# Layer 0's message sum: the one-hots of every fourth group made by ScalarE in place of VectorE

## Chip, core and metric

One core of a Trainium2 chip runs the whole program. The metric is the device time of one execution in microseconds (us); lower is better.

## What is computed

The program is two graph layers over N = 6250 nodes (256 features) and E = 100000 edges. Layer 0 is an attention with six kinds of edges, layer 1 an attention over all edges and self loops. The change lies in one step of layer 0, the sum of weighted messages into their target nodes. In the reference it is this (`w` is the softmax weight, one per edge and head, and the sum over relations follows):

```python
hsum = jax.ops.segment_sum(w[:, :, None] * val_e, seg, num_segments=S)
...
t = (t_rel * present[..., None].astype(x.dtype)).sum(1) / nrel[:, None]
```

`w * val_e` has 256 numbers per edge (4 heads of 64), and the weights themselves are summed as 4 more columns.

## The kernel before, in words

Edges are sorted by target node and cut into visits. A visit is 256 edges (two tiles of 128) that all add into one block of 128 nodes; there are 440 visits. `sum_messages` works on turns of 16 tiles, so 8 visits (t = 0 to 7) in 4 groups (g = 0 to 3) of four tiles, and there are 55 turns. The first turn is written out, the other 54 are a hardware loop. In each turn:

- **SP** loads the value rows of each group, 128x1024 numbers, into `vrows` (line 1174). A group's buffer is loaded again as soon as its values have been weighed, and the four groups are loaded in order, so the load of g = 1 stands behind that of g = 0, and g = 3 behind g = 2.
- **Weigh** (line 1157) multiplies the rows by the weights into `wv`. VectorE weighs groups 0 and 2, GpSimd groups 1 and 3. It waits for the load and for TensorE to be done with the same group of the turn before, since `wv` has one buffer per group.
- **Hot** (line 1263) makes the one-hots of the group's four tiles on VectorE: a 128x512 comparison of a ramp (`iota`) with each edge's place in its block (`dr`). It goes to `vhot`.
- **Beside** (line 1184) copies the weights into the last columns of `wv` on ScalarE.
- **Visit** (line 1237) is two accumulating matmuls of a one-hot (128x128) with weighed rows (128x260, fp32) into one of four PSUM banks. Visit t waits for hot, weigh and beside of its group, in this order, and then for the add of visit t-4, which frees its bank.
- **Add** (line 1256) puts a visit's bank onto the running sum, on VectorE: `run = run * same + psM`. It waits for the visit and for the add before it.
- **Keep** (line 1196) copies each running sum into the accumulator of its node block, on ScalarE.

The order is written out by hand in each engine's program. On VectorE a turn is: weigh 0, hot 0, adds 4 and 5 of the turn before, hot 1, adds 6 and 7 of the turn before, weigh 2, hot 2, adds 0 and 1, hot 3, adds 2 and 3. On ScalarE: beside 0, keeps 4 and 5 (turn before), beside 1, keeps 6 and 7 (turn before), beside 2, keeps 0 and 1, beside 3, keeps 2 and 3. GpSimd does weigh 1 and weigh 3 alone. A hot of one turn may be overwritten once the visits of its group in the turn before are done (`m_done`).

Layer 1 already makes its one-hots on ScalarE in two steps, |dr - ramp| (line 1780) and relu(1 - that) (line 1788). The edge scores of layer 0 do likewise (lines 886 and 889).

Of the kernel before, what the change touches and what calls it, by code (L numbers as in the profile page):

```python
# [6 lines left out]
P = 128  # L7
# [26 lines left out]
ACT = mybir.ActivationFunctionType  # L34
AX = mybir.AxisListType
ds, ts = bass.ds, bass.ts
# [740 lines left out]
GS = 4  # L777
SLOTS = 4 * GS
# [346 lines left out]
def sum_messages(nc, c, dr, v, layer, weights, nh, acc):  # L1125
# [5 lines left out]
    V8 = SLOTS // 2  # L1131
    with Stage(nc) as tmp:
        def sb(name, shape, dt=F32):
            return tmp.enter_context(nc.sbuf_tensor(f"{name}{L}", shape, dt))

        def sem(name):
            return tmp.sem(f"{name}{L}")
# [2 lines left out]
        rows = sb("vrows", [P, SLOTS, D])  # L1140
        wv = sb("wv", [P, SLOTS, width])
        hot = sb("vhot", [P, SLOTS, P])
        run = sb("run", [P, V8, MSG])
        psW = tmp.enter_context(nc.psum_tensor(f"psW{L}", [P, 2, 1024], F32))
        psM = tmp.enter_context(nc.psum_tensor(f"psM{L}", [P, 4, 512], F32))
        w_in = [sem("w_in0_"), sem("w_in1_")]
        loaded = [sem(f"loaded{g}_") for g in range(4)]
        wv_done = [sem("wv_even_"), sem("wv_odd_")]
        w_tr, w_out, ww_done, hot_done, m_done, run_done, kept = map(sem, (
            "w_tr", "w_out", "ww_done", "vhot_done", "m_done", "run_done", "sum_kept"))  # L1150
        NG = SLOTS // GS

        def weigh(engine, ops, i, g):

            engine.wait_ge(loaded[g], 16 * (i + 1))
            engine.wait_ge(m_done, i * V8 + 2 * g + 2)
            ops.tensor_tensor(  # L1157
                wv[:, g * GS:(g + 1) * GS, 0:D].rearrange("p k (h d) -> p k h d", h=H),
                rows[:, g * GS:(g + 1) * GS].rearrange("p k (h d) -> p k h d", h=H),
                w[:, ts(i * NG + g, GS), 0:H].unsqueeze(3).to_broadcast([P, GS, H, DK]), ALU.mult).then_inc(wv_done[g % 2], 1)  # L1160

        with nc.Block() as block:
            @block.sync
            def _(sp):
                for t in range(CT):
                    if t >= 2:
                        sp.wait_ge(w_tr, t - 1)
                    sp.dma_start(win[:, t % 2], weights.rearrange("h (t c p) -> t c h p", t=CT, p=P)[t]).then_inc(w_in[t % 2], 16)
                with sp.Fori(0, NI) as i:
                    for g in range(NG):  # L1170

                        sp.wait_ge(wv_done[g % 2], i * (NG // 2) + g // 2 + 1)
                        o = dr["val"].rearrange("(i k p) d -> i p k d", k=GS, p=P)[ds(i * NG + g, 1)]
                        sp.dma_start(rows[:, g * GS:(g + 1) * GS], o.rearrange("o p k d -> (o p) k d")).then_inc(loaded[g], 16)

            @block.scalar
            def _(act):
                act.sem_inc(kept, V8)
                act.wait_ge(w_out, CT)

                def beside(i, g):

                    act.wait_ge(m_done, i * V8 + 2 * g + 2)
                    nc.scalar.copy(wv[:, g * GS:(g + 1) * GS, D:width], w[:, ts(i * NG + g, GS)]).then_inc(ww_done, 1)

                regs = [act.alloc_register(f"sblk{t}") for t in range(4)]

                def keep(i, visits):
                    if visits[0] % 4 == 0:
                        act.load(regs, v["blk"][0:1, ds(i * V8 + visits[0], 4)])  # L1190
                    for t in visits:
                        V = i * V8 + t
                        blk = act.snap(regs[t % 4], min_val=0, max_val=NB - 1)
                        act.wait_ge(run_done, V + 5)
                        act.wait_ge(kept, V + V8)
                        nc.scalar.copy(acc[:, ds(blk, 1)].rearrange("p o d -> p (o d)"), run[:, t]).then_inc(kept, 1)  # L1196

                def turn(i, first=False):

                    for g in range(NG):  # L1200
                        beside(i, g)
                        if g >= 2:
                            keep(i, (2 * g - 4, 2 * g - 3))
                        elif not first:
                            keep(i - 1, (2 * g + 4, 2 * g + 5))
                turn(0, True)
                with act.Fori(1, NI) as i:
                    turn(i)
                keep(NI - 1, range(4, V8))

            @block.gpsimd
            def _(pool):
                pool.sem_inc(wv_done[1], NG // 2)
                pool.wait_ge(w_out, CT)
                with pool.Fori(0, NI) as i:
                    for g in range(1, NG, 2):
                        weigh(pool, nc.gpsimd, i, g)

            @block.tensor
            def _(pe):  # L1220
                pe.sem_inc(m_done, V8)
                for t in range(CT):
                    pe.wait_ge(w_in[t % 2], 16 * (t // 2 + 1))
                    if t >= 2:
                        pe.wait_ge(w_out, t - 1)
                    for h in range(nh):
                        ins = nc.tensor.transpose(psW[:, t % 2, h * P:h * P + CW], win[:, t % 2, h], c["ident"][0:CW, 0:CW])
                    ins.then_inc(w_tr, 1)
                with pe.Fori(0, NI) as i:
                    for t in range(V8):  # L1230
                        if t % 2 == 0:
                            pe.wait_ge(hot_done, i * NG + t // 2 + 1)
                            pe.wait_ge(wv_done[t // 2 % 2], (i + 1) * (NG // 2) + t // 4 + 1)
                            pe.wait_ge(ww_done, i * NG + t // 2 + 1)
                        pe.wait_ge(run_done, i * V8 + t + 1)
                        for j in range(2):
                            ins = nc.tensor.matmul(psM[:, t % 4, 0:width], hot[:, 2 * t + j], wv[:, 2 * t + j], start=(j == 0), stop=(j == 1))  # L1237
                        ins.then_inc(m_done, 1)

            @block.vector  # L1240
            def _(dve):
                dve.sem_inc(wv_done[0], NG // 2)
                for t in range(CT):
                    dve.wait_ge(w_tr, t + 1)
                    nc.vector.tensor_copy(w[:, t * CW:(t + 1) * CW].rearrange("p c h -> p h c"),
                                          psW[:, t % 2].rearrange("p (h c) -> p h c", c=P)[:, 0:nh, 0:CW]).then_inc(w_out, 1)
                dve.sem_inc(run_done, 3)
                nc.vector.memset(run[:], 0.0).then_inc(run_done, 1)
                dve.wait_ge(w_out, CT)

                def add(i, t):
                    V = i * V8 + t
                    dve.wait_ge(m_done, V + 1 + V8)
                    dve.wait_ge(run_done, V + 4)
                    dve.wait_ge(kept, V + 1)
                    nc.vector.scalar_tensor_tensor(out=run[:, t, 0:width], in0=run[:, (t - 1) % V8, 0:width], scalar=v["same"][:, ds(V, 1)],  # L1256
                                                   in1=psM[:, t % 4, 0:width], op0=ALU.mult, op1=ALU.add).then_inc(run_done, 1)
                def turn(i, first=False):
                    for g in range(NG):
                        if g % 2 == 0:  # L1260
                            weigh(dve, nc.vector, i, g)
                        dve.wait_ge(m_done, i * V8 + 2 * g + 2)
                        nc.vector.tensor_tensor(hot[:, g * GS:(g + 1) * GS], c["iota"][:].unsqueeze(1).to_broadcast([P, GS, P]),  # L1263
                                                v["dr"][:, ts(i * NG + g, GS)].unsqueeze(2).to_broadcast([P, GS, P]),
                                                ALU.is_equal).then_inc(hot_done, 1)

                        if g >= 2:
                            add(i, 2 * g - 4)
                            add(i, 2 * g - 3)
                        elif not first:  # L1270
                            add(i - 1, 2 * g + 4)
                            add(i - 1, 2 * g + 5)
                turn(0, True)
                with dve.Fori(1, NI) as i:
                    turn(i)
                for t in range(V8 - 4, V8):
                    add(NI - 1, t)
# [973 lines left out]
```

## Time and profile before

| | us |
|---|---|
| median of 3 runs | 4758.05 |
| lowest and highest run | 4743.52, 4765.12 |
| profiled execution, its own time | 4761.29 |
| its span in the trace | 4758.8 |
| the sum of layer 0 in it, first weigh to last add | 2365.8 to 2948.4 |

The span is the time from the first to the last instruction. PE is TensorE (PEld its weight loads), DVE is VectorE, ACT is ScalarE, POOL is GpSimd, SP issues the loads. Busy time is counted per instruction, and a name like L1263 is a line of the kernel before. In the timeline a row is one instruction or a run of equal ones (x2, x8); a visit shows as 4 matmul rows, so x8 is two visits.

### The profile page before, as it was taken

The page shows a single profiled execution, that of the slowest core. Times are in us where ns is not written, and L with a number is a line of the kernel's source. Part 1 is how long each engine was busy: PE and PEld are TensorE (multiplying, and loading weights), DVE is VectorE, ACT ScalarE, POOL GpSimd, SP SyncE. Part 2 cuts the span into 40 slices and gives each one's busy share as a digit, 9 for nine tenths or more (in the row PEclk, how much of TensorE's full clock was granted, in tenths as well). Part 3 has the DMA queues.
Part 4 walks back from the last instruction along what each step waited for, and adds up shares of the span by engine and source line. Part 5 has one row for each costly group of instructions (what it writes and reads, how often), then busy time and mean ns, then how long its engine had stood idle before and what let it go on. Part 6 is the DMA issues. An engine that isn't in the chain of part 4 may idle for free. (4 is left out here: it accounts for less than half of the span.)

```text
span 4758.8 us, 56459 instructions
## 1 busy us (share of the span) xinstructions
PE 2853.5 (60%) x10779; PEld 1822.5 (38%) x10780; DVE 3061.9 (64%) x6090; ACT 1481.4 (31%) x3656; POOL 2084.0 (44%) x2102
## 2 busy tenths in 40 slices
PE   0799997666666674000177776766355666556632
PEld 0455554433334342000155554434244444445421
DVE  5333334555555554999899998676366666666665
ACT  0122223333333332231033333434234433434302
POOL 1000005777777774000033333222577777777550
PEclk9999998777877777555599999899677777777765
DMA  4344447999999997000155554000466666666531
GB/s 154 111 137 137 140 140 253 315 312 316 315 314 315 314 315 247 0 0 0 66 197 200 201 196 151 15 18 17 108 188 193 191 185 191 192 189 193 158 122 54
DMA packets 648045, 815.90 MB, mean 171 GB/s; under 512 B 155094, under 2 KB 552310, under 8 KB 647602
## 3 DMA queue, kind: packets, MB, share of 16 engines
q1 hardware_dynamic: 532228, 457.32, 30.0%
q0 software_dynamic: 115696, 357.28, 24.7%
q8 instruction: 38, 0.62, 0.1%
q14 instruction: 83, 0.68, 0.0%
HBM read 541.33 MB, written 274.25 MB: 171 GB/s over the span
## 5 line engine op out<-in xcount | busy, mean ns | idle before, releaser
L821 POOL DMA_INDIRECT rows<-kv,kvi x880 | 832.7, 946 | 890.9 <-DVEq L893 623.0
L1721 POOL DMA_INDIRECT g_rows<-x1t,srci x880 | 848.8, 965 | 286.3 <-issue 259.4
L866 PE MATMUL psD<-qs,hot 128*128 x1760 | 702.9, 525 | 247.7 <-DVE prod L907 193.3
L907 DVE TENSOR_TENSOR prod<-rows,psD 128x256 f32<-128x256 f32 x880 | 363.6, 417 | 465.4 <-DMA rows<-kv,kvi 353.9
L1875 PE MATMUL g_psM<-g_rows,g_hot 128*128 128x264 f32 x1760 | 570.8, 479 | 77.5 <-DVE g_rows L1993 71.0
L1157 POOL TENSOR_TENSOR wv<-vrows,wgt 128x1024 f32<-128x1024 f32 x110 | 219.5, 1996 | 840.0 <-DMA vrows<-val_v 622.3
L866 PEld LDWEIGHTS psD<-qs,hot 128*128 128x128 f32 x1760 | 381.6, 252 | 521.0 <-issue 309.6
L1237 PE MATMUL psM<-wv,vhot 128*128 128x260 f32 x1760 | 445.7, 397 | 138.4 <-DVE run L1256 131.5
L1875 PEld LDWEIGHTS g_psM<-g_rows,g_hot 128*128 128x128 f32 x1760 | 390.0, 233 | 171.9 <-issue 94.2
L1237 PEld LDWEIGHTS psM<-wv,vhot 128*128 128x128 f32 x1760 | 318.1, 190 | 265.9 <-DVE run L1256 219.3
L886 ACT ACTIVATE off<-psB,npiota 128x256 f32<-128x256 f32 x440 | 207.7, 472 | 669.8 <-PE psB L857 667.8
L901 DVE TENSOR_REDUCE sc<-prod 128x4 f32<-128x256 f32 x880 | 357.3, 411 | 0.0
L733 PE MATMUL psKV<-wkv,hT 128*128 128x512 f32 x588 | 302.3, 596 | 0.0
L1788 ACT ACTIVATE g_hot<-g_far 128x512 f32<-128x512 f32 x220 | 138.5, 630 | 520.1 <-PE g_psZ L1864 474.3
L1196 ACT COPY acc<-run 128x264 f32 x440 | 181.3, 412 | 367.7 <-DVE run L1256 366.9
L1780 ACT ACTIVATE g_far<-iota,dr 128x128 f32<-128x128 f32 x880 | 278.0, 386 | 14.8 <-PEq L69 14.8
L1993 DVE TENSOR_TENSOR g_rows<-g_rows,g_psW 128x1024 f32<-128x1024 f32 x220 | 265.6, 1207 | 0.0
L1929 DVE TENSOR_REDUCE g_e<-g_psD 128x128 f32<-128x384 f32 x55 | 30.6, 557 | 361.9 <-DMA g_rows<-x1t,srci 361.9
L1885 PE MATMUL g_psZ<-ident,g_z 128*64 128x128 f32 x55 | 23.0, 418 | 381.7 <-DVE g_z L1935 359.2
L1256 DVE SCALAR_TENSOR_TENSOR run<-run,same,psM 128x260 f32<-128x260 f32 x440 | 211.0, 480 | 35.2 <-DVE run L1256 12.3
L685 DVE COPY qs<-psQ 128x256 f32 (+1 forms) x49 | 20.8, 425 | 329.8 <-PE psQ L737 329.8
L1263 DVE TENSOR_TENSOR vhot<-iota,dr 128x512 f32<-128x512 f32 x220 | 232.0, 1055 | 0.0
(359 smaller groups left out, 4634.8 us busy)
## 6 DMA issues: line engine op xcount, KB each, us to landing
val_v<-rows SPq DMA_DIRECT2D x220, 512.0 KB, 5.0
vrows<-val_v SPq DMA_DIRECT2D x220, 512.0 KB
kv<-stage SPq DMA_DIRECT2D x98, 768.0 KB, 4.7
sums_v<-g_run SPq DMA_DIRECT2D x110, 528.0 KB, 3.6
g_drow<-drow_v SPq DMA_DIRECT2D x55, 512.0 KB
rows<-kv,kvi POOLq DMA_INDIRECT x880, 5.0
g_rows<-x1t,srci POOLq DMA_INDIRECT x880
g_ndt<-nodeb SPq DMA_DIRECT2D x440, 6.0 KB
```

The costliest lines, as they stand in the source:

```text
L733: mm(psKV[:], hT[:, m % 2, t, g], wkv[:, g, t], start=(t == 0 and g == 0), stop=False)
L821: nc.gpsimd.indirect_dma_start(out=rows[:, k], out_offset=None, in_=table, in_offset=bass.IndirectOffsetOnAxis(ap=index[:, i * SLOTS + k:i ...
L866: nc.tensor.matmul(psD[:, k % 4, 0:cols], hot[:, t % 2, j * P:(j + 1) * P], node[:, ds(blk[t], 1)].rearrange("p o d -> p (o d)"), start=Tr ...
L901: nc.vector.tensor_reduce(sc[:, k], prod[:, k % 4].rearrange("p (h d) -> p h d", h=H), AX.X, ALU.add).then_inc(sc_done, 1)
L907: ins = nc.vector.tensor_tensor(prod[:, k % 4], rows[:, k, 0:D], psD[:, k % 4, 0:D], ALU.mult)
L1157: ops.tensor_tensor(wv[:, g * GS:(g + 1) * GS, 0:D].rearrange("p k (h d) -> p k h d", h=H), rows[:, g * GS:(g + 1) * GS].rearrange("p k (h ...
L1237: ins = nc.tensor.matmul(psM[:, t % 4, 0:width], hot[:, 2 * t + j], wv[:, 2 * t + j], start=(j == 0), stop=(j == 1))
L1263: nc.vector.tensor_tensor(hot[:, g * GS:(g + 1) * GS], c["iota"][:].unsqueeze(1).to_broadcast([P, GS, P]), v["dr"][:, ts(i * NG + g, GS)]. ...
L1721: nc.gpsimd.indirect_dma_start(out=rows[:, i % NBUF, k, 0:ROW1], out_offset=None, in_=dr["x1t"], in_offset=bass.IndirectOffsetOnAxis(ap=v[ ...
L1780: ins = nc.scalar.activation(far[:, n % 2, k], c["iota"][:], ACT.Abs, scale=-1.0, bias=v["dr"][:, K:K + 1])
L1875: ins = nc.tensor.matmul(psM[:, V % 4, 0:MSG], hot[:, 2 * t + j], rows[:, i % NBUF, 2 * t + j], start=(j == 0), stop=(j == 1))
L1993: tt(out, out, w.unsqueeze(3).to_broadcast([P, GRP, H, DK]), ALU.mult).then_inc(wv_done, 1)
```

## The change

ScalarE makes the one-hots of group 3 of each turn, by a new function `places`; VectorE no longer does hot 3. `places` writes |dr - ramp| of four tiles into a new buffer `vfar`, one tile at a time (128x128 each), waits for its own last write and for TensorE's visits of the turn before, and then writes relu(1 - vfar) for the group at once (128x512). It stands on ScalarE ahead of beside 2. TensorE waits for a semaphore of its own before visits 6 and 7.

```diff
+        far = sb("vfar", [P, GS, P])
...
+                def places(i):
+                    g = NG - 1
+                    for k in range(GS):
+                        ins = nc.scalar.activation(far[:, k], c["iota"][:], ACT.Abs, scale=-1.0, bias=v["dr"][:, ds(i * SLOTS + (g * GS + k), 1)])
+                    ins.then_inc(far_done, 1)
+                    act.wait_ge(far_done, i + 1)
+                    act.wait_ge(m_done, i * V8 + 2 * g + 2)
+                    nc.scalar.activation(hot[:, g * GS:(g + 1) * GS], far[:], ACT.Relu, bias=1.0, scale=-1.0).then_inc(last_hot, 1)
+
                 def turn(i, first=False):
 
                     for g in range(NG):
+                        if g == 2:
+                            places(i)
                         beside(i, g)
...
-                            pe.wait_ge(hot_done, i * NG + t // 2 + 1)
+                            if t // 2 < NG - 1:
+                                pe.wait_ge(hot_done, i * (NG - 1) + t // 2 + 1)
+                            else:
+                                pe.wait_ge(last_hot, i + 1)
...
-                        dve.wait_ge(m_done, i * V8 + 2 * g + 2)
-                        nc.vector.tensor_tensor(hot[:, g * GS:(g + 1) * GS], c["iota"][:].unsqueeze(1).to_broadcast([P, GS, P]),
+                        if g < NG - 1:
+                            dve.wait_ge(m_done, i * V8 + 2 * g + 2)
+                            nc.vector.tensor_tensor(hot[:, g * GS:(g + 1) * GS], c["iota"][:].unsqueeze(1).to_broadcast([P, GS, P]),
```

```order
L1195 REGISTER_ALU
L1196 ISA
L1196 COPY acc<-run 128x264
L1183 REGISTER_ALU
L1184 ISA
L1184 COPY wv<-wgt 128x4x4
```

The same place with the change, from the last of the four vfar steps to beside 2:

```order
L1202 ISA
L1202 ACTIVATE vfar<-iota,dr 128x128
L1204 REGISTER_ALU
L1205 REGISTER_ALU
L1206 ACTIVATE vhot<-vfar 128x512
L1184 REGISTER_ALU
L1185 ISA
L1185 COPY wv<-wgt 128x4x4
```

Five engine instructions now stand between keep 7 and beside 2: four vfar steps and one vhot step.

VectorE in the loop, before, from add 1 to add 2 (vhot is hot 3):

```order
L1256 SCALAR_TENSOR_TENSOR run<-run,same,psM 128x260
L1262 REGISTER_ALU
L1263 ISA
L1263 TENSOR_TENSOR vhot<-iota,dr 128x512
L1253 REGISTER_ALU
L1255 REGISTER_ALU
L1256 ISA
L1256 SCALAR_TENSOR_TENSOR run<-run,same,psM 128x260
```

The same place with the change:

```order
L1271 SCALAR_TENSOR_TENSOR run<-run,same,psM 128x260
L1268 REGISTER_ALU
L1270 REGISTER_ALU
L1271 ISA
L1271 SCALAR_TENSOR_TENSOR run<-run,same,psM 128x260
```

Add 2 follows add 1 directly; adds 0 to 3 are now four in a row.

## Rows read from the trace of the kernel before

**Rows 1.** Page of the kernel before: totals by engine; granted TensorE clock in 40 slices.
```profile
PE 2853.5 (60%) x10779; PEld 1822.5 (38%) x10780; DVE 3061.9 (64%) x6090; ACT 1481.4 (31%) x3656; POOL 2084.0 (44%) x2102
...
PEclk9999998777877777555599999899677777777765
```

**Rows 2.** Windows view, inside the sum: us, busy of PE, PEld, DVE, ACT, POOL; clock, DMA, GB/s.
```profile
2600.00:2650.00 50.00, 38.29 (x153) 27.20 (x153) 46.38 (x68) 18.05 (x57) 19.34 (x10) 1.00 0.57 192
```

**Rows 3.** Groups by line within the sum of layer 0: busy us, mean ns | idle before, releaser.
```profile
L1263 DVE TENSOR_TENSOR vhot<-iota,dr 128x512 f32<-128x512 f32 x220 | 232.0, 1055 | 0.0
```

**Rows 4.** Timeline of one turn of the sum: start us, us, instruction [idle before <-releaser].
```profile
2599.54 1.22 DVE L1157 TENSOR_TENSOR wv<-vrows,wgt 128x1024 f32<-128x1024 f32 x1
...
2600.68 0.68 DVE L1263 TENSOR_TENSOR vhot<-iota,dr 128x512 f32<-128x512 f32 x1
...
2601.06 2.07 POOL L1157 TENSOR_TENSOR wv<-vrows,wgt 128x1024 f32<-128x1024 f32 x1 [3.22 <-PE psM L1237]
...
2602.39 1.28 DVE L1263 TENSOR_TENSOR vhot<-iota,dr 128x512 f32<-128x512 f32 x1
...
2603.60 1.10 DVE L1256 SCALAR_TENSOR_TENSOR run<-run,same,psM 128x260 f32<-128x260 f32 x2
...
2604.12 2.02 PE L1237 MATMUL psM<-wv,vhot 128*128 128x260 f32 x8 [0.29 <-DVE run L1256]
...
2604.61 1.22 DVE L1157 TENSOR_TENSOR wv<-vrows,wgt 128x1024 f32<-128x1024 f32 x1
2604.89 0.41 ACT L1196 COPY acc<-run 128x264 f32 x1 [0.21 <-DVE run L1256]
2605.21 0.20 ACT L1184 COPY wv<-wgt 128x16 f32 x1
...
2606.35 1.10 DVE L1256 SCALAR_TENSOR_TENSOR run<-run,same,psM 128x260 f32<-128x260 f32 x2
2606.44 1.90 POOL L1157 TENSOR_TENSOR wv<-vrows,wgt 128x1024 f32<-128x1024 f32 x1 [3.31 <-PE psM L1237]
...
2606.88 2.02 PE L1237 MATMUL psM<-wv,vhot 128*128 128x260 f32 x8 [0.74 <-DVE run L1256]
...
2607.36 1.53 DVE L1263 TENSOR_TENSOR vhot<-iota,dr 128x512 f32<-128x512 f32 x1
...
2608.81 1.09 DVE L1256 SCALAR_TENSOR_TENSOR run<-run,same,psM 128x260 f32<-128x260 f32 x2
...
2609.34 2.02 PE L1237 MATMUL psM<-wv,vhot 128*128 128x260 f32 x8 [0.44 <-DVE run L1256]
...
2610.05 1.22 DVE L1157 TENSOR_TENSOR wv<-vrows,wgt 128x1024 f32<-128x1024 f32 x1
...
2611.61 2.03 POOL L1157 TENSOR_TENSOR wv<-vrows,wgt 128x1024 f32<-128x1024 f32 x1 [3.26 <-PE psM L1237]
...
2616.96 1.90 POOL L1157 TENSOR_TENSOR wv<-vrows,wgt 128x1024 f32<-128x1024 f32 x1 [3.33 <-DMA vrows<-val_v]
```

**Rows 5.** Timeline, start of the sum: a weigh of VectorE beside one of GpSimd.
```profile
2376.68 1.90 POOL L1157 TENSOR_TENSOR wv<-vrows,wgt 128x1024 f32<-128x1024 f32 x1 [4.82 <-PE psM L1237]
2376.94 2.72 DVE L1157 TENSOR_TENSOR wv<-vrows,wgt 128x1024 f32<-128x1024 f32 x1
```

**Rows 6.** Timeline, layer 1: the same two ScalarE steps.
```profile
3965.18 1.26 ACT L1780 ACTIVATE g_far<-iota,dr 128x128 f32<-128x128 f32 x4
...
3966.47 0.63 ACT L1788 ACTIVATE g_hot<-g_far 128x512 f32<-128x512 f32 x1
```

**Rows 7.** Timeline, layer 0's scores: ScalarE's Abs, Relu, and the matmul behind them.
```profile
1713.82 0.47 ACT L886 ACTIVATE off<-psB,npiota 128x256 f32<-128x256 f32 x1 [3.42 <-PE psB L857]
...
1714.41 0.42 ACT L889 ACTIVATE hot<-off 128x256 f32<-128x256 f32 x1
...
1715.06 1.13 PE L866 MATMUL psD<-qs,hot 128*128 x4 [1.11 <-ACT hot L889]
```

**Rows 8.** Timeline, last turn of the sum: four visits in one go.
```profile
2943.90 3.77 PE L1237 MATMUL psM<-wv,vhot 128*128 128x260 f32 x16 [0.74 <-DVE run L1256]
```

More of the change, by code:

```diff
@@ L1148, in sum_messages @@
         wv_done = [sem("wv_even_"), sem("wv_odd_")]
-        w_tr, w_out, ww_done, hot_done, m_done, run_done, kept = map(sem, (
-            "w_tr", "w_out", "ww_done", "vhot_done", "m_done", "run_done", "sum_kept"))
+        w_tr, w_out, ww_done, hot_done, far_done, last_hot, m_done, run_done, kept = map(sem, (
+            "w_tr", "w_out", "ww_done", "vhot_done", "vfar_done", "vhot_last", "m_done", "run_done", "sum_kept"))
         NG = SLOTS // GS
@@ L1261, in turn @@
                             weigh(dve, nc.vector, i, g)
-                        dve.wait_ge(m_done, i * V8 + 2 * g + 2)
-                        nc.vector.tensor_tensor(hot[:, g * GS:(g + 1) * GS], c["iota"][:].unsqueeze(1).to_broadcast([P, GS, P]),
-                                                v["dr"][:, ts(i * NG + g, GS)].unsqueeze(2).to_broadcast([P, GS, P]),
-                                                ALU.is_equal).then_inc(hot_done, 1)
+                        if g < NG - 1:
+                            dve.wait_ge(m_done, i * V8 + 2 * g + 2)
+                            nc.vector.tensor_tensor(hot[:, g * GS:(g + 1) * GS], c["iota"][:].unsqueeze(1).to_broadcast([P, GS, P]),
+                                                    v["dr"][:, ts(i * NG + g, GS)].unsqueeze(2).to_broadcast([P, GS, P]),
+                                                    ALU.is_equal).then_inc(hot_done, 1)
                         if g >= 2:
```

## The prediction

> **What bounds the kernel now.** The page comes first: no engine is busy over the whole span (VectorE 64%, TensorE 60%), so the stage decides [rows 1]. The change touches the sum of layer 0 alone, so I read that stretch in the windows view: VectorE 46.4 of 50 us, TensorE 38.3, GpSimd 19.3, ScalarE 18.1, DMA 57%, granted clock 1.00, which is the upper of its two levels, 2.4 GHz [rows 2]. VectorE is the bound, and in the groups view its costliest group there is hot (L1263), 232.0 us in 220 instructions, none of which it waited idle for [rows 3]. Its mean is 1055 ns though a single one takes 0.68 us. The timeline of a turn says why [rows 4].
>
> A turn starts with weigh 0 at 2599.54 and the next with 2610.05: **10.51 us**. Hot 0 takes 0.68. Hot 1 starts at 2602.39 while GpSimd weighs group 3 (2601.06 to 2603.13) and ends at 2603.67, 0.54 after GpSimd. Hot 3 starts at 2607.36 while GpSimd weighs group 1 (2606.44 to 2608.34) and ends at 2608.89, 0.55 after it. At the start of the sum weigh 2 ends at 2379.66, 1.08 after GpSimd's 2378.58, in place of taking 1.22 [rows 5]. So a VectorE instruction that reads two SBUF tensors stands still while a GpSimd weigh runs; adds, which read one operand from PSUM, do not (the pair at 2606.35 takes 1.10 beside GpSimd, the pair at 2608.81 1.09 without). The other way round, GpSimd's weigh at 2601.06 began during hot 0 and took 2.07 in place of 1.90 [rows 4].
>
> **What the change does, part by part.** I write times from H, the end of hot 1 in a turn (2603.67 in rows 4).
>
> (a) *Removed from VectorE: hot 3.* From add 1 to add 2 now passes one add step, 0.62 (a pair of 1.10 less one add of 0.48), where it was 2608.81 - 2606.35 - 0.62 = 1.84. VectorE is **1.22 us** earlier per turn if nothing else holds it, 54 x 1.22 = 66 us. Its next hot 1 could start at: add 0 at H + 2.68 (2606.35), add 3 three steps later at + 4.54, next weigh 0 0.62 later at + 5.16 (1.24 from add 2 to weigh 0 in rows 4, less one step), hot 1 2.85 after that (2602.39 - 2599.54): **H + 8.01**. Unblocked, that hot ends at + 8.69, a turn of 8.7.
>
> (b) *Added to ScalarE, ahead of beside 2.* The same two steps in layer 1 cost 1.26 for four Abs and 0.63 for the Relu [rows 6]. The wait between them here is of the kind of L886 to L889, 0.12 from end to start [rows 7]. Keep 7 starts at H + 1.22 (2604.89), and what follows it starts 0.32 later (2605.21) [rows 4]. So Abs from + 1.54 to + 2.80, Relu + 2.92 to + 3.55, beside 2 from + 3.46 (a copy starts 0.09 ahead of the last one's end, as 2605.21 does) to + 3.66. ScalarE has room for it in total (1.9 us per turn on top of 18 in 50), but not at this place: TensorE's visit 4 needs beside 2 and started at H + 3.21 (2606.88).
>
> (c) *Visit 4 now waits for ScalarE.* From beside 2's end to the matmul I have 0.05 (add to matmul, 2606.83 to 2606.88 [rows 4]) and 0.23 (Relu to matmul, 1714.83 to 1715.06 [rows 7]) as bounds; TensorE's sequencer has one step between, the second row has two, so I take 0.17: visit 4 at + 3.83, 0.62 later than before. Queued behind it on TensorE are visits 5, 6 and 7, and nothing holds them now: add 2 ends at + 4.4, and beside 3, behind keeps 0 and 1, at about + 5.1, before visit 6 at + 5.6. Four visits in one go take 3.77 against 2.02 for two [rows 8, 4], so 1.75 more; GpSimd's weigh 3 starts 2.27 after the start of a pair of visits 6 and 7 (2609.34 to 2611.61 [rows 4]). It waits for visit 7, since wv has one buffer. So GpSimd starts weigh 3 at 3.83 + 1.75 + 2.27 = **H + 7.85**.
>
> (d) *The load of its rows.* Where DMA released GpSimd it was 5.69 after the end of the VectorE weigh that freed the pair of buffers (2611.27 to 2616.96 [rows 4]). For weigh 3 that is weigh 2, which ends at + 2.16 (2605.83): also + 7.85. The loads no longer have slack here.
>
> (e) *What meets what.* GpSimd at H + 7.85, hot 1 at H + 8.01. By 0.16 us GpSimd is first; hot 1 stands for the whole weigh: 7.85 + 1.90 + 0.54 = **10.29** from H to H. The turn is thus set by a ring: hot 1, add 7, keep 7, Abs and Relu, beside 2, visits 4 to 7, weigh 3, hot 1. VectorE's 1.22 us are given back as 1.60 of standing behind GpSimd where it was 0.60. Gain 10.51 - 10.29 = 0.22 per turn, 54 x 0.22 = 12 us.
>
> Weigh 1 does not matter: visit 2 starts at + 0.45, GpSimd follows 2.32 later (2604.12 to 2606.44 [rows 4]) at + 2.77, just when hot 2 is done, and is through at + 4.67, beside adds alone. TensorE waits for one semaphore in place of another. No DMA is added. The new buffer only fills SBUF.
>
> **The sum.** 4761.3 - 12 = 4749 against the profiled execution's own time (its span is 4758.8), which lies 3 us above the median of the runs; as a median that is **4746**.
>
> The Trainium skill (ScalarE: Activation LUTs, section Rules for kernel authors) advises VectorE, not ScalarE, for relu, max or add. By it the group would have stayed on VectorE and the gain would be nil, which is a case inside the chance of no change below. By the rows the direct prices are 1.9 us of ScalarE for 0.68 to 1.53 of VectorE, and what decides is which engine the ring passes through. The trace agrees with the rule as far as prices go.
>
> **The rivals.**
>
> *1. Hot 1 gets in first.* The 0.16 us are the difference of two chains of eight terms, each good to some hundredths; one Abs step longer or visit 4 at the upper bound (+ 0.06) and a late load (+ 0.08) already use it up. Then hot 1 ends at + 8.69, GpSimd waits for it and holds weigh 2 instead, up to 0.70 late. That turn takes 8.69, the next meets a load that is 0.70 later (weigh 2 frees it), GpSimd at 8.55 against hot 1 at 8.71, and takes 10.99 if GpSimd is first again: a mean of 9.84; or every turn takes 9.4 if not. Gain 36 to 60 us: 4698 to 4722, say 4715. A more expensive ScalarE part thus makes the kernel faster. The Trainium skill (SBUF — State Buffer, section SBUF: two separate sides) calls the shared ports an exclusive lock that goes to whoever starts first, for the whole instruction; the trace agrees that it is exclusive, by the 0.54 and 1.08 after GpSimd's end [rows 4, 5], but no row of this trace shows a near tie. A mix of both kinds of turn gives a time between.
>
> *2. All of VectorE's saving stays.* If GpSimd kept its place in the turn, a turn would be 10.51 - 1.22 = 9.29: 4692. For it: ScalarE and TensorE have idle time. Against it: weigh 3 cannot start before visit 7, and VectorE runs ahead of it.
>
> *3. ScalarE's detour becomes the bound: slower.* From add 7's end, keep 7 0.19 later, 0.32 + 1.26 + 0.12 + 0.63 - 0.09 + 0.20 to beside 2's end, 0.17, four visits 3.77, and add 7 of the next turn about 0.6 later: 7.2 us round. It decides from 3.4 us more per turn, that is if an Abs whose bias address comes from a register cost 1.2 in place of 0.4. At 4 us more the turn is 11.2: 4761 + 54 x 0.65 = 4796. Against it: L1184 sets addresses in the loop too and still starts 0.32 after keep 7.
>
> *4. The change does not do what it says*: if hot 3 stayed on VectorE nothing would move. The order in the program shows it gone.
>
> **How the numbers follow.** About 0.5%, 24 us, is what a measurement of this kernel can tell from no change. Forecast, GpSimd first throughout or nearly (gain 2 to 22): 0.52. Rival 1 with mixes: 0.37. Rival 2: 0.05. Rival 3: 0.04. The rest (0.02) is a small loss. Hence faster 0.42, same 0.53, slower 0.05. The forecast's own range is 4736 to 4758. The range for 8 in 10 has to take in most of rival 1: 4700 to 4763.
>
> **What would show it.** In the profile after: hot x165, mean near 1.2 us (0.68, 0.68 and 2.2 to 2.3 in a turn), where rival 1 shows hot 1 at 0.68 and weigh 2 at 1.9; weigh 0 every 10.3 us (rival 1: 8.7 to 9.8); TensorE idle in front of visit 4 put down to beside 2 (L1185) and visits 4 to 7 as one row x16; GpSimd starting 0.1 to 0.3 us ahead of hot 1; L1202 0.385 and L1206 0.63. VectorE nearly as busy as before though it does less. Wrong would be: hot 1 short in most turns, GpSimd released by DMA later than + 8.0, or a granted clock below 1.00 in the sum.

## The result, and the profile after

| | before | with the change |
|---|---|---|
| median of 22 runs, us | 4761.24 | 4749.02 |
| span of the profiled execution, us | 4758.8 | 4745.0 |
| the sum of layer 0, VectorE's first weigh to last add, us | 581.7 | 572.7 |

The ratio is **0.9978, 95% interval 0.9969 to 0.9986**: 0.2% faster, 7 to 15 us. That is below the 0.5% which the prediction took for the least that can be told from no change, but 22 runs of each do tell it. The forecast was 4746. One of the 22 runs with the change took 5579.66 us at a mean granted clock of 0.706, against 0.78 to 0.80 in the others, and has no part in the ratio.

The sum is counted here from VectorE's first weigh. The 2365.8 given above for the kernel before is GpSimd's first weigh, 0.8 us earlier.

Page of the changed kernel, totals by engine and granted TensorE clock, and the windows view of 50 us inside the sum (the columns as in [rows 2]):

```profile
PE 2829.3 (60%) x10779; PEld 1825.1 (38%) x10780; DVE 3035.5 (64%) x6035; ACT 1579.7 (33%) x3931; POOL 2073.0 (44%) x2102
...
PEclk9999998877777876555599998999677777777765
```

```profile
2600.00:2650.00 50.00, 37.56 (x154) 28.23 (x155) 44.66 (x65) 26.52 (x81) 18.96 (x10) 1.00 0.63 210
```

VectorE is busy 44.7 of 50 us, hardly less than the 46.4 of [rows 2], though it no longer makes a quarter of the one-hots. ScalarE went from 18.1 to 26.5. The clock stays at 1.00, its upper level of 2.4 GHz.

Groups by line within the sum, the changed kernel (busy us, mean ns | idle before):

```profile
L1252 PE MATMUL psM<-wv,vhot 128*128 128x260 f32 x1760 | 430.8, 393 | 144.5 <-DVE run L1271 135.4 <-DVE vhot L1279 6.9
...
L1202 ACT ACTIVATE vfar<-iota,dr 128x128 f32<-128x128 f32 x220 | 70.1, 389 | 0.0
...
L1206 ACT ACTIVATE vhot<-vfar 128x512 f32<-128x512 f32 x55 | 34.6, 630 | 6.2
```

There are 165 hots where there were 220 [rows 3], but one costs 1196 ns on average where it was 1055: 232.0 us of VectorE became 197.3, not 174. Abs and Relu cost what layer 1 pays for them [rows 6].

Timeline of one turn of the changed kernel, from hot 1 to hot 1:

```profile
2605.42 2.23 DVE L1279 TENSOR_TENSOR vhot<-iota,dr 128x512 f32<-128x512 f32 x1
...
2607.57 1.10 DVE L1271 SCALAR_TENSOR_TENSOR run<-run,same,psM 128x260 f32<-128x260 f32 x2
...
2608.58 1.22 DVE L1158 TENSOR_TENSOR wv<-vrows,wgt 128x1024 f32<-128x1024 f32 x1
...
2609.18 1.27 ACT L1202 ACTIVATE vfar<-iota,dr 128x128 f32<-128x128 f32 x4
...
2610.32 1.10 DVE L1271 SCALAR_TENSOR_TENSOR run<-run,same,psM 128x260 f32<-128x260 f32 x2
...
2610.57 0.63 ACT L1206 ACTIVATE vhot<-vfar 128x512 f32<-128x512 f32 x1
2611.10 0.19 ACT L1185 COPY wv<-wgt 128x16 f32 x1
...
2611.42 5.84 PE L1252 MATMUL psM<-wv,vhot 128*128 128x260 f32 x24 [1.30 <-DVE run L1271]
...
2611.71 1.11 DVE L1271 SCALAR_TENSOR_TENSOR run<-run,same,psM 128x260 f32<-128x260 f32 x2 [0.29 <-DVE run L1271]
...
2612.96 1.23 DVE L1158 TENSOR_TENSOR wv<-vrows,wgt 128x1024 f32<-128x1024 f32 x1
...
2615.53 1.90 POOL L1158 TENSOR_TENSOR wv<-vrows,wgt 128x1024 f32<-128x1024 f32 x1 [3.30 <-DMA vrows<-val_v]
2615.81 2.17 DVE L1279 TENSOR_TENSOR vhot<-iota,dr 128x512 f32<-128x512 f32 x1
```

H is 2607.65, the end of the first hot. This is the ring of part (e) of the prediction. Hot 1 ends, weigh 2 ends at H + 2.15, and ScalarE's Abs start at + 1.53, its Relu at + 2.92; beside 2 ends at + 3.64 and visit 4 starts at + 3.77. GpSimd starts weigh 3 at **H + 7.88**, hot 1 starts 0.28 later at H + 8.16, stands still and ends at 2617.98, 0.55 after GpSimd. The turn is **10.33 us**, where the one shown of before was 10.51 [rows 4]. Two things to read with care: the row of TensorE (x24: visits 4 to 7, then 0 and 1) names the add as what released it, and the add had ended at 2610.80; what came last is beside 2 (2611.29). And GpSimd was released by its load (DMA), as 53 of the 55 weighs 3 in this trace were; before, 53 of 55 were released by a visit, the two of [rows 4] among them.

The turns differ by some hundredths, so the means over the 52 turns from the third on are the better measure: **10.36** with the change, 10.53 before. In both kernels hot 1 ends behind weigh 3, so the mean turn has three terms, from H to weigh 3, weigh 3 itself, and 0.55 to the end of hot 1. Before they are 7.93 + 2.05 + 0.55, with the change 7.91 + 1.90 + 0.55. So the ring was already closed before the change, there through hot 3, adds 2 and 3 and visits 6 and 7. And 0.15 of the 0.17 us gained per turn lies in weigh 3, which no longer begins while hot 0 runs (2.07 in [rows 4], 1.90 here).

### The profile page after: what moved, and what is told of

It reads as the page before. It is cut to its first block and busy times, and to the rows that moved or that the text cites. A ratio compares the mean times of both kernels' runs of the same rounds, so it can differ in the third digit from the quotient of the medians.

```text
span 4745.0 us, 56951 instructions
## 1 busy us (share of the span) xinstructions
PE 2829.3 (60%) x10779; PEld 1825.1 (38%) x10780; DVE 3035.5 (64%) x6035; ACT 1579.7 (33%) x3931; POOL 2073.0 (44%) x2102
## 5 line engine op out<-in xcount | busy, mean ns | idle before, releaser
L1252 PE MATMUL psM<-wv,vhot 128*128 128x260 f32 x1760 | 430.8, 393 | 144.5 <-DVE run L1271 135.4
L889 ACT ACTIVATE hot<-off 128x256 f32<-128x256 f32 x440 | 183.2, 416 | 50.0
```

## Experiments

All times are medians in us, beside runs of the kernel before on the same chip, whose medians were 4761.39 (made_once, loads, once_loads, abs6) and 4763.26 (abs5, before_moved, hot1_moved, moved_early). "The sum" is the time from VectorE's first weigh to the end of the last add in the profiled execution, and "mean turn" the mean of the 52 turns from the third on, from the end of one hot 1 to the next, in the same execution. The text below each run reads single turns, which lie up to 0.1 us off it (in abs6 more).

| run | time | ratio to before, 95% | the sum | mean turn |
|---|---|---|---|---|
| before | 4761.24 | | 581.7 | 10.53 |
| changed kernel | 4749.02 | 0.9978 (0.9969 to 0.9986) | 572.7 | 10.36 |
| made_once | 4753.09 | 0.9977 (0.9967 to 0.9988) | 573.4 | 10.36 |
| loads | 4746.38 | 0.9962 (0.9948 to 0.9977) | 564.3 | 10.19 |
| once_loads | 4713.61 | 0.9890 (0.9866 to 0.9913) | 534.0 | 9.63 |
| abs5 | 4758.84 | 0.9993 (0.9981 to 1.0005) | 579.3 | 10.49 |
| abs6 | 4746.36 | 0.9971 (0.9953 to 0.9988) | 564.7 | 10.21 |
| before_moved | 4718.91 | 0.9902 (0.9886 to 0.9919) | 540.3 | 9.76 |
| hot1_moved | 4694.76 | 0.9853 (0.9837 to 0.9870) | 509.6 | 9.16 |
| moved_early | 4694.41 | 0.9853 (0.9834 to 0.9873) | 507.9 | 9.16 |

The theory is the ring of the prediction: the turn is fixed by GpSimd's weigh 3, which is due at a fixed time after hot 1 and blocks the next hot 1. The rivals: ScalarE's detour sets the turn by itself; the loads do; VectorE's work does.

### made_once: is ScalarE's work what holds the turn?

```diff
-                        if g == 2:
+                        if g == 2 and first:
                             places(i)
...
-                                pe.wait_ge(last_hot, i + 1)
+                                pe.wait_ge(last_hot, 1)
```

> Group 3's one-hots are made in the first turn only, so 54 turns use those of the first: VectorE's part of the change without ScalarE's work. If ScalarE's detour alone sets the turn: weigh 3 starts at H + 7.2, turn 9.7, about 4716. If the loads of weigh 3's rows (weigh 2's end at H + 2.15, 5.73 to landing) set it as well: turn 10.33, about 4749, no gain at all from taking the work away.

This kernel leaves out the making of group 3's one-hots in 54 of the 55 turns: visits 6 and 7 use those of the first turn.

Measured: 4753.09, and the same mean turn. Two hots, weigh 2, TensorE and GpSimd in its timeline:

```profile
2598.17 2.21 DVE L1279 TENSOR_TENSOR vhot<-iota,dr 128x512 f32<-128x512 f32 x1
...
2601.32 1.22 DVE L1158 TENSOR_TENSOR wv<-vrows,wgt 128x1024 f32<-128x1024 f32 x1
...
2603.59 3.77 PE L1252 MATMUL psM<-wv,vhot 128*128 128x260 f32 x16 [0.74 <-DVE run L1271]
...
2608.33 1.90 POOL L1158 TENSOR_TENSOR wv<-vrows,wgt 128x1024 f32<-128x1024 f32 x1 [3.36 <-DMA vrows<-val_v]
2608.54 2.24 DVE L1279 TENSOR_TENSOR vhot<-iota,dr 128x512 f32<-128x512 f32 x1
```

With H = 2600.38, visit 4 starts at H + 3.21 as in the kernel before, so ScalarE's detour is gone, and nothing is gained: GpSimd starts at + 7.95 (7.91 on average, as in the changed kernel), released by the load, 5.79 after weigh 2's end (2602.54). ScalarE's detour is not what the change lost its gain to, or not alone.

### loads: do the loads hold it?

```diff
-                    for g in range(NG):
+                    for g in (0, 1, 3, 2):
                         ...
                         sp.wait_ge(wv_done[g % 2], i * (NG // 2) + g // 2 + 1)
```

> The changed kernel with SP's loads in the order 0, 1, 3, 2, so that the rows of weigh 3 no longer stand behind weigh 2. If two rings tie (loads at H + 7.88, ScalarE and TensorE at H + 7.79): turn 10.24, about 4744. If the loads alone held the turn: 9.7 and about 4716.

Measured: 4746.38, turn 10.19. Hot 1, GpSimd's weigh 3, hot 1:

```profile
2602.64 2.03 DVE L1279 TENSOR_TENSOR vhot<-iota,dr 128x512 f32<-128x512 f32 x1
...
2612.42 1.91 POOL L1158 TENSOR_TENSOR wv<-vrows,wgt 128x1024 f32<-128x1024 f32 x1 [3.16 <-PE psM L1252]
...
2612.83 2.04 DVE L1279 TENSOR_TENSOR vhot<-iota,dr 128x512 f32<-128x512 f32 x1
```

H is 2604.67 and GpSimd starts at + 7.75, now released by visit 7. So two chains run to nearly the same point, the load at + 7.91 on average and ScalarE with visits 4 to 7 at + 7.75 (7.74 on average). Taking away the second gains nothing, taking away the first only the 0.17 us between them.

### once_loads: both chains cut

The two edits above together (so this kernel, too, leaves out group 3's one-hots after the first turn).

> Both edits: group 3's one-hots made in the first turn only, and loads in the order 0, 1, 3, 2. Two-ring theory: neither ring holds any more, GpSimd starts weigh 3 at H + 7.2, turn 9.7, about 4716, though each edit alone gave 0 to 5 us. If something third sets the turn: near 4749 still.

Measured: 4713.61. Hot 1, weigh 3, hot 1:

```profile
2600.96 1.48 DVE L1279 TENSOR_TENSOR vhot<-iota,dr 128x512 f32<-128x512 f32 x1
...
2609.62 1.91 POOL L1158 TENSOR_TENSOR wv<-vrows,wgt 128x1024 f32<-128x1024 f32 x1 [2.60 <-PE psM L1252]
...
2610.59 1.48 DVE L1279 TENSOR_TENSOR vhot<-iota,dr 128x512 f32<-128x512 f32 x1
```

GpSimd starts at H + 7.18 (H = 2602.44) and the turn is 9.63 = 7.18 + 1.90 + 0.55. One edit alone gave the sum nothing, the other 8 us, and both 39. Hot 1 takes 1.48: it still stands, only for less long.

### abs5 and abs6: a longer ScalarE part

```diff
-        far = sb("vfar", [P, GS, P])
+        far = sb("vfar", [P, GS + 2, P])
...
-                    for k in range(GS):
+                    for k in range(GS + 2):
...
-... hot[:, g * GS:(g + 1) * GS], far[:], ACT.Relu ...
+... hot[:, g * GS:(g + 1) * GS], far[:, 0:GS], ACT.Relu ...
```

(abs6; abs5 has GS + 1. The extra steps take the bias of tile k % GS.)

> One more Abs step per turn (output not used), 0.29 us: weigh 3 due at H + 8.1, hot 1 at H + 8.16. GpSimd still first in most turns: turn 10.4 to 10.5, about 4756, slower than the changed kernel; the kernel with two more steps is faster than this one. If the time simply falls with every turn in which hot 1 wins, and it wins some here: 4745 to 4756.

> Two more Abs steps per turn on ScalarE (their output is not used), 0.59 us later at visit 4. The race theory: GpSimd's weigh 3, due at H + 8.4, now comes after hot 1 (H + 8.16 in the changed kernel), so hot 1 is not blocked in at least every other turn: mean turn 9.9, about 4730, faster than the changed kernel although it does more. Rival, ScalarE's chain sets the turn and what is added to it is added to the time: mean turn 10.8, about 4776. Rival, only the loads of weigh 3's rows set the turn: 4749, no change from the changed kernel.

Timeline of abs5, weigh 3 and hot 1, then TensorE from visit 4 and the next weigh 3:

```profile
2600.48 1.90 POOL L1158 TENSOR_TENSOR wv<-vrows,wgt 128x1024 f32<-128x1024 f32 x1 [3.45 <-PE psM L1252]
2600.61 2.32 DVE L1279 TENSOR_TENSOR vhot<-iota,dr 128x512 f32<-128x512 f32 x1
...
2607.00 4.22 PE L1252 MATMUL psM<-wv,vhot 128*128 128x260 f32 x18 [1.59 <-ACT wv L1185]
...
2610.97 1.90 POOL L1158 TENSOR_TENSOR wv<-vrows,wgt 128x1024 f32<-128x1024 f32 x1 [3.45 <-PE psM L1252]
```

H is 2602.93 and GpSimd starts at + 8.04, before hot 1 by 0.13 us as in the turn shown (2600.48 and 2600.61). It is first in every turn, and the turn is 10.49, 8.04 + 1.90 + 0.55. Weigh 3 is later by the whole added step than the + 7.75 to which ScalarE's chain led in the run loads. Against the changed kernel, whose weigh 3 waited for the load until + 7.91, only 0.13 of the 0.29 us counts: the sum is 7 us longer and the runs 10, which makes the kernel equal to before.

Timeline of abs6, two turns:

```profile
2605.36 2.17 DVE L1279 TENSOR_TENSOR vhot<-iota,dr 128x512 f32<-128x512 f32 x1
...
2611.88 7.28 PE L1252 MATMUL psM<-wv,vhot 128*128 128x260 f32 x32 [1.89 <-ACT wv L1185]
...
2615.68 0.68 DVE L1279 TENSOR_TENSOR vhot<-iota,dr 128x512 f32<-128x512 f32 x1
2615.85 2.27 POOL L1158 TENSOR_TENSOR wv<-vrows,wgt 128x1024 f32<-128x1024 f32 x1 [3.74 <-PE psM L1252]
...
2617.30 1.90 DVE L1158 TENSOR_TENSOR wv<-vrows,wgt 128x1024 f32<-128x1024 f32 x1
```

and the weigh 3 and hot 1 that follow:

```profile
2624.93 1.91 POOL L1158 TENSOR_TENSOR wv<-vrows,wgt 128x1024 f32<-128x1024 f32 x1 [3.32 <-DMA vrows<-val_v]
2625.21 2.17 DVE L1279 TENSOR_TENSOR vhot<-iota,dr 128x512 f32<-128x512 f32 x1
```

H is 2607.53. Hot 1 starts at 2615.68, 0.17 us before GpSimd, and takes 0.68; now GpSimd stands (2.27 in place of 1.90) and holds weigh 2 (1.90 in place of 1.22). That turn takes 8.83. Weigh 2 ends late (2619.20), its load is late, and weigh 3 comes at the new H + 8.57, again ahead of hot 1: that turn takes 11.02. The mean of this pair is 9.93, as expected (9.9), and short and long turns alternate through the whole sum. But the mean turn of the sum is 10.21. So 0.30 us more on ScalarE per turn makes the sum 15 us *shorter* than in abs5, and 8 us shorter than in the changed kernel. The runs order the two in the same way (4746 against 4759), and don't tell abs6 from the changed kernel. The whole missed its 4730 by 16 us. Most of that is TensorE's clock, which falls 11 times within the sum of abs6. Windows of 2 us of abs6:

```profile
2464.00:2466.00 2.00, 1.45 (x7) 0.93 (x5) 2.00 (x4) 1.80 (x7) 0.34 (x1) 1.00 0.01 2
2466.00:2468.00 2.00, 0.66 (x3) 0.61 (x4) 1.44 (x4) 1.65 (x6) 1.57 (x1) 0.99 0.66 185
2468.00:2470.00 2.00, 2.00 (x7) 1.52 (x6) 1.86 (x3) 1.41 (x5) 0.00 (x0) 0.50 0.97 336
2470.00:2472.00 2.00, 2.00 (x8) 1.62 (x7) 1.59 (x4) 0.83 (x3) 0.00 (x0) 0.65 0.38 126
```

TensorE had been busy 1.45 and 0.66 of 2 us before the granted clock fell to 0.50, its lower level of 1.2 GHz, and came back within the 2470 window. Its idle time before visit 4 was 1.89 us in abs6 (at the end of the row of 2611.88), against 1.30 in the changed kernel, whose windows of 50 us show 1.00 up to 2900. In abs6 they show 0.93 to 1.00. The wait of 1.88 to 1.89 us comes in every second turn, 26 times; the clock fell behind 11 of them, within 0.7 us of TensorE's restart, and stayed at 1.00 behind the other 15. After a fall the visits are late, hot 1 is through long before weigh 3, and weigh 2 takes 2.48. Of the 26 pairs of turns, the 16 without a fall take 19.9 us and the 10 with one 21.2. Eleven falls at 1.3 us make 14 of the 16 us. What decides whether the clock falls behind such a wait is open.

### hot1_moved: the ring cut on VectorE

```diff
-                        if g < NG - 1:
-                            dve.wait_ge(m_done, i * V8 + 2 * g + 2)
+                        for gg in ((0, 1), (), (2,), ())[g]:
+                            dve.wait_ge(m_done, i * V8 + 2 * gg + 2)
```

(and gg for g in the instruction below)

> The changed kernel with hot 1 moved on VectorE to right behind hot 0, so that it is done before GpSimd starts weigh 3, whose 1.9 us then lie beside adds 4 to 7, which it cannot block. Ring theory (hot 1 behind weigh 3 closes the ring): the ring is cut, turn near VectorE's own 9.0 to 9.1 us, about 4685. Rival, the turn is set by the engines' work in the ring and not by the block: weigh 3's end, visits and ScalarE stay, turn 10.2 to 10.3, about 4749.

Timeline, VectorE from weigh 0 to weigh 0, and weigh 3 on GpSimd:

```profile
2600.33 1.23 DVE L1158 TENSOR_TENSOR wv<-vrows,wgt 128x1024 f32<-128x1024 f32 x1
...
2601.47 1.28 DVE L1279 TENSOR_TENSOR vhot<-iota,dr 128x512 f32<-128x512 f32 x2
...
2602.68 0.48 DVE L1271 SCALAR_TENSOR_TENSOR run<-run,same,psM 128x260 f32<-128x260 f32 x1
2602.95 1.91 POOL L1158 TENSOR_TENSOR wv<-vrows,wgt 128x1024 f32<-128x1024 f32 x1 [2.96 <-DMA vrows<-val_v]
...
2604.09 1.10 DVE L1271 SCALAR_TENSOR_TENSOR run<-run,same,psM 128x260 f32<-128x260 f32 x2 [0.23 <-DVE run L1271]
...
2605.11 1.22 DVE L1158 TENSOR_TENSOR wv<-vrows,wgt 128x1024 f32<-128x1024 f32 x1
...
2609.49 1.23 DVE L1158 TENSOR_TENSOR wv<-vrows,wgt 128x1024 f32<-128x1024 f32 x1 [0.15 <-issue]
```

Hots 0 and 1 are done at 2602.75 and GpSimd starts weigh 3 at 2602.95; until 2604.86 VectorE has adds alone, and weigh 2 starts at 2605.11. No hot is blocked from the third turn on. The turn is 9.16 (2600.33 to 2609.49), 4694.76: the loads, ScalarE's five steps and visit 4's delay are all still there. That is 68.5 us below before and far from the rival's 4749; it is also 10 us above the 4685 expected.

The second turn has a closer start than abs5 or abs6. Hots 0 and 1 are the x2:

```profile
2381.61 1.28 DVE L1279 TENSOR_TENSOR vhot<-iota,dr 128x512 f32<-128x512 f32 x2
2382.20 2.46 POOL L1158 TENSOR_TENSOR wv<-vrows,wgt 128x1024 f32<-128x1024 f32 x1 [1.59 <-PE psM L1252]
```

GpSimd's weigh starts at 2382.20, while hot 0 runs and 0.02 us ahead of hot 1. Yet hot 1 takes its plain 0.68, and GpSimd takes 2.46 in place of 1.90 and ends 1.76 after it: behind a hot that is already running, the next hot got in ahead of GpSimd.

### before_moved: the same reordering without the change

```diff
-                        dve.wait_ge(m_done, i * V8 + 2 * g + 2)
+                        for gg in ((0, 1), (), (2, 3), ())[g]:
+                            dve.wait_ge(m_done, i * V8 + 2 * gg + 2)
```

> The kernel before with the same reordering and nothing else: VectorE makes all four hots, hot 1 right behind hot 0 and hot 3 right behind hot 2, so both GpSimd weighs fall beside four adds. If the block is what cost 0.60 and 0.85 us per turn: turn 9.5 to 9.7, about 4712, better than the change alone. If VectorE's plain work is the bound: 10.5, 4761.

Timeline, VectorE's weighs and pairs of hots, and GpSimd's weighs:

```profile
2601.01 1.23 DVE L1157 TENSOR_TENSOR wv<-vrows,wgt 128x1024 f32<-128x1024 f32 x1
...
2602.15 1.28 DVE L1264 TENSOR_TENSOR vhot<-iota,dr 128x512 f32<-128x512 f32 x2
...
2602.95 2.25 POOL L1157 TENSOR_TENSOR wv<-vrows,wgt 128x1024 f32<-128x1024 f32 x1 [2.74 <-PE psM L1237]
...
2605.79 1.22 DVE L1157 TENSOR_TENSOR wv<-vrows,wgt 128x1024 f32<-128x1024 f32 x1
...
2606.93 1.28 DVE L1264 TENSOR_TENSOR vhot<-iota,dr 128x512 f32<-128x512 f32 x2
2607.91 2.06 POOL L1157 TENSOR_TENSOR wv<-vrows,wgt 128x1024 f32<-128x1024 f32 x1 [2.72 <-PE psM L1237]
...
2610.77 1.22 DVE L1157 TENSOR_TENSOR wv<-vrows,wgt 128x1024 f32<-128x1024 f32 x1
```

The four hots take 2 x 1.28 where they take 4.2 on average before (4 x 1055 ns, [rows 3]), and GpSimd waits a little instead (2.25 and 2.06). The turn is 9.76 (9.5 to 9.7 were expected) and the time 4718.91, 7 us above the 4712 expected. Against 4763.26 that is 44 us for a change of order, over three times what moving the work to ScalarE gave.

### moved_early: ScalarE's Abs out of the way

The four Abs are issued after beside 1, ahead of keeps 6 and 7; the Relu stays ahead of beside 2.

> hot1_moved, and ScalarE's four Abs moved up to where it waits for adds 6 and 7, so that only the Relu stands ahead of beside 2. If ScalarE's detour still delays visit 4 enough to matter once the ring is cut: faster than hot1_moved by 10 to 20 us. Ring theory: VectorE is the bound of both, equal within 5 us, about 4685.

Measured: 4694.41 against 4694.76, both with turns of 9.16, and not the 10 to 20 us less by which ScalarE's detour would have shown. With the ring cut, ScalarE's place doesn't matter.

## Why the prediction was right

- **The lost gain.** Forecast: 1.22 us of VectorE per turn, 1.00 of it given back in hot 1, a turn of 10.29 and 12 us. Measured: hot 1 takes 2.13 to 2.30 from the third turn on (1.28 in [rows 4]), the mean turn is 10.36, the sum 9 us shorter and the runs 12 us. So the ring is borne out. That the 12 was met to the microsecond is luck: the sum holds 9 of it, and the rest lies inside the interval of 7 to 15. hot1_moved shows how much the block held back: with hot 1 out of GpSimd's reach the sum is 63 us shorter than in the changed kernel, the rest of the change untouched.
- **"VectorE is the bound"** was too simple a reading of the kernel before. Its 46.4 of 50 us contain the standing of hots 1 and 3, and the turn was set by weigh 3 there too (7.93 + 2.05 + 0.55). The forecast came out right because part (e) counted the turn through weigh 3 all the same. One row is misnamed in it: the weigh that ends at 2379.66 [rows 5] is weigh 0 of the second turn, not weigh 2; the 1.08 stands.
- **Visit 4** was put at H + 3.83 and started at + 3.77. From beside 2's end it is 0.13, between the bounds of 0.05 and 0.23.
- **Weigh 3** was put at H + 7.85 by ScalarE and TensorE and at + 7.85 by the load. They are + 7.75 (run loads) and + 7.91 on average (7.84 to 7.97, short of the + 8.0 that would have been a sign of being wrong). That the two were level was part (d), but the text drew the ring through ScalarE. In the changed kernel it is the load that comes last, and made_once shows that the ring closes through weigh 2 and its load without ScalarE's part.
- **Hot 1** was put at H + 8.01 and came at + 8.16. The term that was too small is the row of four adds: I counted three steps of 0.62, and add 2 starts 1.39 after add 0 (2610.32, 2611.71). The profile puts 0.29 of idle before it down to the add before. GpSimd's lead was therefore 0.25 on average (0.15 to 0.32), not 0.16, and rival 1 was further off than that number said.
- **Rival 1** said that a more expensive ScalarE part makes the kernel faster, with turns of 8.69 and 10.99. abs6 shows turns of 8.83 and 11.02 where the clock stays up, and abs5, one step short of it, the slow side. That whoever starts first runs through holds in abs5 and abs6 down to leads of 0.13 (GpSimd) and 0.17 us (VectorE), which bears out the exclusive lock of the Trainium skill (SBUF — State Buffer, section SBUF: two separate sides). In the closer start of hot1_moved, with hot 0 still running, it was not the one whose record starts first that ran first, and there the measurement decides.
- **Rival 2** needed weigh 3 to keep its place in the turn. It moved with the ring. **Rival 3** needed an Abs of 1.2 us; it took 0.39. **Rival 4** falls with the 165 hots.
- **The ScalarE rule** (ScalarE: Activation LUTs, section Rules for kernel authors, in the Trainium skill) would have kept relu and its like on VectorE. The prices agree with it, 1.9 us against 0.68; but with the block out of the way, hot1_moved beats before_moved by 0.60 us per turn, 31 us of the sum and 24 us between the medians of four runs each, so here giving the group to ScalarE is worth something after all.

## What to carry to other kernels

When an engine is slowed by another one's instructions, taking work off it only shifts the moment at which the two meet. Look first for which instructions can't be blocked (here the adds, with an operand in PSUM), and put them where the other engine runs: this was worth 44 us without moving any work, and made the move of work worth 24 more. And when two waits end within 0.2 us of each other, cut both before calling either harmless.

## What the runs showed of the hardware

- Between VectorE instructions with two SBUF inputs and a GpSimd tensor_tensor, whoever started 0.13 to 0.17 us earlier ran through and the other stood: a hot of 0.68 took 2.32, GpSimd's 1.90 took 2.27. The blocked hot ended 0.54 to 0.55 after GpSimd in every such turn. In the second turn of hot1_moved, a GpSimd weigh that started while hot 0 ran let hot 1 right behind it go first too, and took 2.46. The adds, with one operand in PSUM, took 0.48 beside GpSimd and without it.
- TensorE's granted clock fell to 0.50 in the middle of a stage in which TensorE is busy for three quarters of the time, when its idle time in one place of a turn grew from 1.30 to 1.89 us: 11 times behind 26 such waits, at 1.3 us each. With 1.59 us in that place (abs5) it stayed at 1.00. This is seen in one kernel, and no run isolates what sets it off.
- Still open: what sets the 9.16 of hot1_moved, 10 us above its forecast as a whole, where VectorE is idle for 0.23 us before two of its adds (one in the rows shown) and GpSimd is released by its load.
